# A two-layer attention and feed-forward kernel with a written instruction order: where the token rows, the first q tiles, wo and the softmax denominators go, under a new set of ranks

## What is computed

```python
x = hidden_states                                  # (8, 256, 512)
xn = layernorm(x)
x = x + attn0(xn) @ Wo + lora_experts(xn)          # 32 heads of 16, one shared k and v, ALiBi, causal
xn = layernorm(x)
x = x + attn1(xn) + ffn(xn)                        # attn1: softmax over the 16 features of a token
# ffn: down(silu(gate(xn)) * up(xn)), 512 -> 1792 -> 512, integer weights with a scale per row
```

## Time and profile before

| | us |
|---|---|
| three executions, median | 640.08 |
| lowest and highest | 638.49, 640.99 |
| the profiled execution's own time | 638.76 |
| its span, first to last instruction | 636.9 |
| TensorE busy | 587.7 (92%) |
| VectorE busy | 479.8 (75%) |
| ScalarE busy | 373.4 (59%) |
| GpSimd busy | 352.3 (55%) |

### The profile page before, as it was taken

One profiled execution on the slowest core, in us unless ns is written; L12 is line 12 of the kernel. 1 busy time (PEld: TensorE's weight loads), 2 busy tenths in 40 slices (PEclk: granted clock), 3 DMA queues, 4 the chain that ended last, 5 costly groups with the idle time before them and its releaser, 6 DMA issues.

```text
span 636.9 us, 14221 instructions
## 1 busy us (share of the span) xinstructions
PE 587.7 (92%) x5582; PEld 437.5 (69%) x5582; DVE 479.8 (75%) x1050; ACT 373.4 (59%) x695; POOL 352.3 (55%) x363
## 2 busy tenths in 40 slices
PE   5767956699999999999999999999999999999997
PEld 3746623566886688756877587867885877785783
DVE  4687999799989599968789649994787468654642
ACT  3343769747755586555848475756564886652240
POOL 4332779434646487546548654765575776652230
PEclk9977985799999999999999999999999999999999
DMA  9869698601310143012500150005100100000000
GB/s 243 107 133 186 165 216 194 79 2 38 52 18 5 67 104 33 4 33 68 69 3 3 43 94 2 3 15 97 10 3 22 48 1 1 34 3 1 34 1 33
DMA packets 38290, 36.11 MB, mean 57 GB/s; under 512 B 8912, under 2 KB 28272, under 8 KB 38224
## 3 DMA queue, kind: packets, MB, share of 16 engines
q1 hardware_dynamic: 29488, 24.41, 18.9%
q0 software_dynamic: 2720, 8.49, 6.5%
q10 hardware_dynamic: 6016, 2.31, 1.5%
HBM read 30.28 MB, written 8.39 MB: 61 GB/s over the span
## 4 chain that ended last, share of the span: by engine, by line
PE 65%; DVE 21%; issue 5%; DMA 3%; ACT 3%; POOL 2%; SPq 1%; ACTq 0%; DVEq 0%
PE B_bank L1236 24%; PE B_bank L1257 15%; PE A_bank L1188 6%; PE B_bank L1129 4%; PE A_bank L1161 4%; DVE mx L1510 4%; PE A_bank L1095 3%; PE E_bank L1145 3%; PE E_bank L1141 1%; DVE probs L1526 1%; DVE hf L1626 1%; DVE st L1377 1%; DMA q_parts<-qs 1%; DVE nmp L1519 1%; PE B_bank L1224 1%
## 5 line engine op out<-in xcount | busy, mean ns | idle before, releaser
L857 POOL TENSOR_TENSOR probs<-e,probs 128x512 f16<-128x512 f32 x176 | 209.9, 1198 | 151.6 <-ACT probs L980 150.8
L1236 PE MATMUL B_bank<-xs,wgu 128*128 128x256 f16 x1792 | 206.8, 273 | 0.0
L979 ACT ACTIVATE e<-E_bank,wn 128x512 f32<-128x512 f32 x192 | 133.1, 693 | 121.1 <-PE E_bank L1145 56.6
L1236 PEld LDWEIGHTS B_bank<-xs,wgu 128*128 128x128 f16 x1792 | 174.0, 98 | 23.3 <-DVE hf L1616 0.5
L980 ACT ACTIVATE probs<-E_bank,wn 128x512 f16<-128x512 f32 x192 | 133.3, 694 | 0.0
L1257 PE MATMUL B_bank<-wd,hbuf 128*128 128x512 f16 x448 | 100.0, 379 | 1.1 <-DVE hf L1626 1.1
L1510 DVE TENSOR_REDUCE mx<-B_bank 128x8 f32<-128x256 f32 (+6 forms) x168 | 88.0, 579 | 4.9 <-PE B_bank L1129 4.5
L871 POOL TENSOR_TENSOR hbuf<-hf,hbuf 128x512 f16<-128x512 f32 x56 | 66.1, 1181 | 38.9 <-ACT hbuf L1008 38.7
L1257 PEld LDWEIGHTS B_bank<-wd,hbuf 128*128 128x128 f16 x448 | 43.5, 98 | 50.4 <-DVE hf L1626 1.4
L1616 DVE SCALAR_TENSOR_TENSOR hf<-ebuf,B_bank 128x512 f32<-128x512 f32 x56 | 38.2, 683 | 44.4 <-ACT ebuf L1018 44.2
L1129 PE MATMUL B_bank<-kk,qq 128*128 128x32 f16 (+20 forms) x512 | 64.3, 269 | 4.6 <-issue 2.4
(11 more groups left out here) (198 smaller groups left out, 690.7 us busy)
## 6 DMA issues: line engine op xcount, KB each, us to landing
qq<-q_parts SPq DMA_DIRECT2D x21, 256.0 KB
x<-in_x SPq DMA_DIRECT2D x20, 256.0 KB, 3.6
out_y<-x SPq DMA_DIRECT2D x16, 256.0 KB, 2.0
xa<-in_x SPq DMA_DIRECT2D x12, 256.0 KB, 4.7
q_parts<-qs SPq DMA_DIRECT2D x12, 256.0 KB, 2.6
wgu<-in_gate_w POOLq DMA_DIRECT2D x4, 448.0 KB, 7.8
wgu<-in_up_w POOLq DMA_DIRECT2D x4, 448.0 KB, 6.9
wd<-in_down_w POOLq DMA_DIRECT2D x4, 448.0 KB, 6.7
```

The source lines that it names most:

```text
L857: pool.tensor_tensor(probs[:, u % PSLOTS, 1, :], e32[:, w, :], probs[:, u % PSLOTS, 0, :], ALU.subtract).then_inc(s_lop, 1)
L979: act.activation(e32[:, w, :], psum("exp", i, g, w)[:, :], ACT.Exp, scale=wn[:, 7:8])
L1236: mm = pe.matmul(psum(name, u, i)[:, a * SEQ:(a + 1) * SEQ].rearrange("p (t n) -> p t n", t=NU), wgu[:, m, k, (2 * i + a) * P:(2 * i + a + ...
```

## The change

It has six parts.

1. The token rows of batch 1 are written by VectorE, in four more `hot` copies (8 now); SP's 1 MB copy and its semaphore are gone.
2. Each of the eight first q tiles has a slot of its own, `q_first`, that lies in the tile `wd`, which is loaded later. The waits for earlier stores go, in `q0` and in `q` for the tiles behind.
3. wo and the two copies of lora_b are loaded by SP (`wo`), between the constants and the second x chunk; GpSimd's `late` shrinks from 12 to 9 steps.
4. The `ffn_load` steps no longer wait in the plan for the late loads, and those for layer 1 for nothing but batch 0's maxima and split 4. In the order that comes out the splits `lo` 8 and 9 stand before the first `exp` unit of GpSimd.
5. `pv` writes the reciprocals back into the PSUM bank and multiplies from there; the bank comes free with the multiplication, and the semaphore `s_norm` goes.
6. Six of the planner's costs, and all ranks, change; a rank may have a fourth number, for the second chunk's or the first batch's steps alone. `xn0` of chunk 1 waits also for `tok(0, 1)`, which may now come later.

```diff
-            for n in range(12):
-                p.add("POOL", ("late", n), *([] if n < 2 else [sp("gather_first", NK - 1, gap=4.0)] if n < 5
-                                             else [sp("nm", 0), pool("lo", NK)]), at=14.0)
+            for n in range(9):
+                p.add("POOL", ("late", n), *([sp("nm", 0), pool("lo", NK)] if n > 1 else []), at=14.0)
             for n in range(3):
-                p.add("ACT", ("squares2", n), *([pool("late", n + 1, gap=6.0), pool("late", 4, gap=6.0)] if n else [act("squares", NK - 1)]))
+                p.add("ACT", ("squares2", n), *([sp("wo", gap=13.0)] if n else [act("squares", NK - 1)]))
...
+        q_first = wd[:, 0:NB * NK, :].rearrange("p (b m) (a t) -> p b m a t", b=NB, a=2)
-        rden = sb("rden", [P, 2 * HG], F32)
...
+            def wo_load():
+                for dst, source in ((wo_sb[:, 0:NK, :], wo.rearrange(kp, p=P)), (wo_sb[0:NE * LR, NK, :], lora_b),
+                                    (wo_sb[NE * LR:P, NK, :], lora_b)):
+                    sp.dma_start(dst, source).then_inc(s_wo, 16)
-            def hot_rows():
-                sp.wait_ge(s_hotrow, 1)
-                sp.dma_start(qq[R_HOT:P, 1, :, :], hot.unsqueeze(1).broadcast_to([P - R_HOT, NH, SEQ])).then_inc(s_hot[1], 16)
...
             def store(b, m):
                 wait_used(act, "q0", b, m)
-                act.dma_start(q_dram[0, m * P:(m + 1) * P, :, b, :], qs[:, m % 2, :, b * SEQ:(b + 1) * SEQ]).then_inc(s_q0[b][m], 16)
+                act.dma_start(q_dram[0, m * P:(m + 1) * P, :, b, :], q_first[:, b, m, :, :]).then_inc(s_q0[b][m], 16)
...
-                if m >= 2:
-                    act.wait_ge(s_q0[b][m - 2], 16)
-                act.activation(qs[:, m % 2, 0, b * SEQ:(b + 1) * SEQ].rearrange("p (r j) -> p r j", r=TR),
+                act.activation(q_first[:, b, m, 0, :].rearrange("p (r j) -> p r j", r=TR),
...
             def hot_(n):
-                h0 = 8 * n
-                dve.tensor_copy(qq[R_HOT:P, 0, h0:h0 + 8, :], hot.unsqueeze(1).broadcast_to([P - R_HOT, 8, SEQ])).then_inc(s_hot[0], 1)
+                h0 = 8 * (n % 4)
+                dve.tensor_copy(qq[R_HOT:P, n // 4, h0:h0 + 8, :], hot.unsqueeze(1).broadcast_to([P - R_HOT, 8, SEQ]))\
+                   .then_inc(s_hot[n // 4], 1)
...
-                at_least(dve, s_norm, n)
+                if n:
+                    wait_used(dve, "pv", (n - 1) // NHG, (n - 1) % NHG)
                 dve.tensor_reduce(osum[:, :, :], pvb[:, :, 0:2 * HD].rearrange("p n (a d) -> p n d a", a=2),
                                   AX.X, ALU.add)
-                dve.reciprocal(rden[:, :], pvb[:, :, 2 * HD]).then_inc(free("pv", i, g), 1)
-                wait_used(dve, "pv", i, g)
+                link(dve.reciprocal(pvb[:, :, 2 * HD], pvb[:, :, 2 * HD]))
...
-                                  rden[:, :].rearrange("p (t h) -> p t h", t=2).unsqueeze(3)
-                                  .broadcast_to([P, 2, HG, HD]), ALU.mult).then_inc(s_norm, 1)
+                                  pvb[:, :, 2 * HD].rearrange("p (t h) -> p t h", t=2).unsqueeze(3)
+                                  .broadcast_to([P, 2, HG, HD]), ALU.mult).then_inc(free("pv", i, g), 1)
```

Of the table of ranks, two lines before and after:

```diff
-    "POOL": {"start": (148.5, -2, -29), "ffn_load": (-52, 0, 38), "ln0": (177, 0.5, -41), "clear": (83, -1, -17), "norm": (305, 2),
+    "POOL": {"start": (186, 2, -45, -7), "ffn_load": (169, -1, -20, -108), "ln0": (587, 4, -200, -6), "clear": (-316.5, -1, -23, -94),
```

99 lines of the change are left out of this document (44 added, 55 removed), and 24 rows, old and new, of tables (RANK, US).

## The result

The changed kernel takes 643.27 us (median of 20 runs, 639.43 to 647.19), the kernel before 639.92 (20 runs, 637.70 to 643.37): **ratio 1.0052, 95% interval 1.0037 to 1.0067**. It is slower by about 3.3 us, where 638.7 and no change were predicted. The time lies inside the predicted range of 630 to 647; the kernel became slower, by little but with an interval that lies clear of 1, and that was not forecast.

The account below looks back on a forecast made before the run. TensorE was taken as the bound, through when its full stretch begins and the work done by then. Terms -3.3, +3.3 and -1.5 gave -1.5 us on 638.76, scaled to a median of 638.7 us, no change; range 630 to 647.

Parts of the forecast that it names:

- What bounds the kernel: Whole span: TensorE, busy 587.7 of 636.9 us; all hangs on when its full stretch begins and work done by then.
- the full stretch: From 123.2 to 600 us, where TensorE is busy for 469.88 of 476.80 us in the kernel before.
- The slot wait: Early q tiles: the 8.58 us wait until a first q tile has left its slot was to go.
- Step A: Up to VectorE's first maximum reduction, behind GpSimd's all-reduce pause: start at 54.0 instead of 46.40 us, 7.6 later.
- rival 2: Before GpSimd's all-reduce: ScalarE's four stores delay the first low split, deciding from 4.6 us; slower, 644.7 us, chance 0.17.
- Step B: From the first maximum reduction to batch 0's negated maxima: these start at 71.0 us instead of 66.41.
- Step C: From the first negated maxima to batch 2's maxima: less VectorE work and waiting, start at 120.8 us, 3.3 earlier.
- The -3.3 and the +3.3: At batch 2's maxima: start 3.3 us earlier, but 3.3 us of TensorE work not yet done; the two cancel.
- Step D: In the full stretch: lighter VectorE gives -1.5 us, between -5 and 0; new ranks can move it 2 either way.
- Rival 1: Up to batch 2's maxima VectorE hardly waits, and its lighter load gives 4.0 us later: faster, 631.4 us, chance 0.27.
- Rival 3: PV groups: the PSUM bank held 0.4 us longer delays TensorE, deciding from 12 groups; 644 us and more, chance 0.04.
- rival 4: Multiplications by the reciprocals: as costly with one operand in PSUM, so 2.6 and 1.5 us are missing; 642.8, chance 0.04.

Follow-up runs that it names:

- 0.9852: All code edits of the change with each engine's order taken from the kernel before, against the kernel before: ratio 0.9852, 629.98 us.
- 0.9880: The kernel before with the reciprocals written back to PSUM and its orders kept, against the kernel before: ratio 0.9880, 631.86 us.

## Why the prediction was wrong

**What bounds the kernel** was right as to the engine: TensorE's idle and busy time account for every span to a few tenths. That everything hangs on how early the full stretch begins and what is done by then was too much: in the table above, kernels differ by up to 8.5 us in the full stretch's idle time and by up to 7.8 in TensorE's busy time. The slot wait and that for lora_b are gone, as said.

**Step A** was right in its chain and 2.4 us short. The all-reduce was reached at 31.87 (30.7), the pause was 14.7 us (13.6), the first maxima came at 56.35 (54.0). Of ScalarE's first four stores one took 2.42 us where 0.577 was taken; that is the beginning of rival 2, and its delay of 1.2 at the all-reduce is far from the 4.6 from which it was to decide.

**Step B** came out right by luck: 71.0 predicted, 71.20 measured. The stretch from the first maximum to the negated maxima was put at 17.0 us and took 14.85. The 1.3 us for a TensorE that starts at the lower level were not seen, for VectorE hardly waits there (14.61 us busy of 14.85). This error cancelled the 2.4 of step A.

**Step C** failed, and most with what it was to give back. It put batch 2's maxima at 120.8 and they came at 124.42. The stretch from the negated maxima to there, in the kernel before and in the changed one (columns of the earlier trace rows):

```profile
66.41:124.14 57.73, 40.75 (x415) 25.46 (x413) 51.06 (x101) 48.91 (x84) 46.43 (x53) 0.78 0.83 177
```

```profile
71.20:124.42 53.22, 36.64 (x394) 24.51 (x393) 48.25 (x104) 40.94 (x71) 39.91 (x48) 0.74 0.88 182
```

The prediction took off 1.1, 2.6 and 2.4 us of VectorE's work, which left some 45, and 5 us of waits. The waits are 5.0 (53.22 less 48.25), though of another kind: 3.8 in one piece, for the tokens of chunk 1, which TensorE does behind the first exponentials, and these wait for the rows of negated maxima. It was the work that shrank by only 2.8, to 48.25 us. The multiplications took 2.3 as said, and the negated maxima of batch 1 1.03 for the 1.06 said. But batch 0's two instructions took 2.2 us for 0.4, nine probability subtractions 8.5 for 6.9, and four normalisations of x 5.4 for 3.8:

```profile
L1518 DVE TENSOR_TENSOR probs<-e,probs 128x512 f16<-128x512 f32 x9 | 8.5, 944 | 0.0
L1379 DVE TENSOR_SCALAR xa<-xa,mv,rs 128x512 f32<-128x512 f32 x4 | 5.4, 1369 | 0.0
```

These are the same instructions at other lengths. The order is not the only reason: with the reciprocals alone changed and the order kept, the normalisations already took 5.2. And TensorE's deficit at 123.2 us was 5.35 and not 3.3. The -3.3 and the +3.3 were to cancel; in the traces nothing came early, and the deficit is nearly all of the 5.7 us by which the spans differ.

**Step D** failed twice, with opposite signs. What the lighter VectorE gives in the full stretch was taken at 1.5 us; with the reciprocals alone it was 3.9, inside the bounds. "The new ranks can move it by 2 either way" was a guess at the one part that no row bore on; against the old order they cost 3.5 there.

**The sum**, by the runs: the PSUM reciprocals are worth 7.4 to 8 us where 4.1 (2.6 and 1.5) were booked. Without these 4.1 the forecast's -1.5 us is +2.6 for all the rest of the change; it is 11, of which the order is 12.8 and the other code edits about -1.8, by 0.9852 and 0.9880, whose intervals overlap. The step that failed is C, the one from "the first negated maxima are 4.6 us late" to "batch 2's maxima are 3.3 early", with the +2 in D for the ranks: **an engine's busy time was counted through a reordered stretch as if every instruction not named kept its duration**, and all but the reciprocals was booked at 2.6 us, where it cost 11. That the total came as near as 0.7 per cent is luck: the gain of the reciprocals and the cost of the order were both far too small in the sum. The run with 14.0 in the planner's table shows how little the first number says: negated maxima 16.6 us sooner, and 0.5 per cent slower.

**The rivals.** Rival 2 (0.17) named the side and 644.7 us, but its mechanism, four slow stores, is not what happened: one of the four was slow, for a delay of 1.2 us, and starting the negated maxima 16.6 us sooner didn't bring the time back. Rival 1 (0.27) named 631.4, which is near what the edits alone give in the old order, 629.98, but VectorE still has 6.1 us without work in that kernel's stretch C (49.66 busy of 55.73). Rival 3, the held bank, and rival 4, a multiplication as dear as before, are both refuted: 64 times 0.29 us, and 1.2 per cent gained with the bank held.

On the multiplication the Trainium skill (GPSIMD Engine Reference, Specifications) says that GpSimd shares its SBUF interfaces with VectorE, with contention for VectorE's instructions with two SBUF inputs. The runs agree: with both operands in SBUF the longest took 1280, 1285 and 1359 ns in three kernels, with one in PSUM 295 in sixteen. In the kernel before, each of the 35 that took over 350 ns overlaps in time with an instruction of GpSimd, and so do 12 of the 29 shorter ones. The probability subtractions with two SBUF inputs kept their 845 ns in the mean when the reciprocals alone were moved. In the changed code in the old order the first nine took 7.7 us for 6.9, in the changed kernel 8.5: half of their growth in step C is there without the new order.

Open stays which steps of the new order cost the 12.8 us, why its second half loses 4.5 us in small waits, and why the two halves' losses don't add. No run separates single steps there.
